# The mixing stage of a hybrid network written out tile by tile, with another order of steps on TensorE and VectorE

## What is computed

```
t = t + attn(ln(t))
t = t + ffn(ln(t))

def attn(inputs):                      # 8 heads of 16, 64 landmarks
    q, k, v = split(inputs @ Wqkv);  q = q * SCALE
    q_l, k_l = means of q, k over 16 tokens each
    attn1 = softmax(q @ k_l.T)         # 1024 x 64 per head
    attn2 = softmax(q_l @ k_l.T);  attn3 = softmax(q_l @ k.T)
    out = attn1 @ (pinv(attn2) @ (attn3 @ v)) + conv(v)
    return out @ Wout + bout

def ffn(x):                            # 2 shared experts, 8 routed, top 2
    probs = softmax(x @ gate_w.T + gate_b)
    top_v, top_i = top_k(probs, 2);  cw = top_v put at top_i, else 0
    routed = sum over e of cw[e] * (gelu(x @ rw1[e].T + rb1[e]) @ rw2[e].T + rb2[e])
    return shared(x) + sum(sb2) + routed
```

## Time and profile before

| | |
|---|---|
| three timed runs | 3307.7, 3250.42, 3266.44 us; median 3266.44 |
| profiled execution | 3237.99 us, of it the span of the profile 3235.9 us |
| mean granted clock of TensorE | 0.896 |
| PE busy | 2808.2 us (87%) |
| DVE busy | 2358.7 us (73%) |
| ACT busy | 1559.8 us (48%) |
| POOL busy | 1308.9 us (40%) |

### The profile page before, as it was taken

How to read it: one execution, slowest core, us unless ns; L and a number is a source line. 1 busy time by engine, 2 the same in 40 slices (tenths; PEclk the granted TensorE clock), 3 DMA queues, 4 the chain that set the end, 5 groups by cost and what they waited for, 6 DMA issues and landing times. The chain is left out here.

```text
span 3235.9 us, 96795 instructions
## 1 busy us (share of the span) xinstructions
PE 2808.2 (87%) x35815; PEld 2115.9 (65%) x35815; DVE 2358.7 (73%) x6126; ACT 1559.8 (48%) x3112; POOL 1308.9 (40%) x1616
## 2 busy tenths in 40 slices
PE   2999899997998899998888888887881999999998
PEld 1666666665776577777785666665661777767776
DVE  2687978885555688876776777677772877778888
ACT  1566756773443333331003333333330777778887
POOL 0476756774332111110001655555655000027776
PEclk6598969996999899998898987788885999999999
DMA  3011111110222000000000111111112444433333
GB/s 121 21 43 41 43 39 30 53 31 26 66 71 66 27 20 19 19 13 3 4 3 25 50 48 48 38 45 48 44 40 77 94 99 102 100 96 97 102 103 90
DMA packets 282520, 170.58 MB, mean 53 GB/s; under 512 B 94716, under 2 KB 269192, under 8 KB 281864
## 3 DMA queue, kind: packets, MB, share of 16 engines
q1 hardware_dynamic: 265736, 131.53, 14.9%
q0 software_dynamic: 16384, 33.59, 3.6%
HBM read 75.13 MB, written 71.30 MB: 45 GB/s over the span
## 5 line engine op out<-in xcount | busy, mean ns | idle before, releaser
L2303 DVE TENSOR_TENSOR e_glo<-e_g,e_ghi 128x512 f16<-128x512 f32 x540 | 374.8, 696 | 130.0 <-ACT e_ghi L2210 121.7
L2189 POOL DMA_INDIRECT e_got<-ys_dram,e_idx x256 | 254.9, 996 | 484.8 <-DMA ys_dram<-e_yo 401.2
L2205 ACT ACTIVATE e_g<-psum,b 128x512 f32<-128x512 f32 x540 | 371.1, 687 | 153.1 <-PE psum L2359 134.1
L2376 PE MATMUL psum<-w2hi,e_ghi 128*128 (+1 forms) x2160 | 389.8, 219 | 4.8 <-DVE e_glo L2303 4.7
L2378 PE MATMUL psum<-w2lo,e_ghi 128*128 (+1 forms) x2160 | 389.6, 219 | 0.0
L2380 PE MATMUL psum<-w2hi,e_glo 128*128 (+1 forms) x2160 | 389.6, 219 | 0.0
L1738 POOL DMA_INDIRECT xs_dram<-m_xt,m_idxl x256 | 264.3, 1032 | 110.9 <-issue 72.3
L2376 PEld LDWEIGHTS psum<-w2hi,e_ghi 128*128 128x128 f16 x2160 | 211.3, 98 | 73.2 <-DVE e_glo L2303 11.6
L2378 PEld LDWEIGHTS psum<-w2lo,e_ghi 128*128 128x128 f16 x2160 | 211.4, 98 | 60.9
L485 POOL TENSOR_TENSOR pT<-pT,rpbx 128x512 f32<-128x512 f32 x128 | 162.8, 1272 | 197.6 <-ACT pT L533 197.6
L2210 ACT ACTIVATE e_ghi<-psum,b 128x512 f16<-128x512 f32 x334 | 227.3, 680 | 0.0
(11 more groups left out here) (329 smaller groups left out, 7502.5 us busy)
## 6 DMA issues: line engine op xcount, KB each, us to landing
ys_dram<-e_yo SPq DMA_DIRECT2D x71, 256.0 KB
xT<-in_xT SPq DMA_DIRECT2D x16, 512.0 KB, 3.8
xw<-in_x SPq DMA_DIRECT2D x16, 512.0 KB, 5.1
f_xm<-x_dram SPq DMA_DIRECT2D x32, 256.0 KB, 2.9
mid_dram<-f_xm SPq DMA_DIRECT2D x32, 256.0 KB
l_t<-mid_dram SPq DMA_DIRECT2D x16, 512.0 KB
m_t<-mid_dram SPq DMA_DIRECT2D x16, 512.0 KB
res_dram<-m_rest SPq DMA_DIRECT2D x16, 512.0 KB
```

The lines of the kernel that those rows point to most:

```text
L2189: gp.indirect_dma_start(out=got[:, q % 2, k, t, :], out_offset=None, in_=ys, in_offset=bass.IndirectOffsetOnAxis(idx[:, q // 2, i:i + 1], 0))\
L2205: ac.activation(g32[:, c % 4, :], bank(c % 4), ACT.Gelu, bias=bias, scale=1.0 / WSCALE)\
L2303: ve.tensor_tensor(glo[:, c % 4, :], g32[:, c % 4, :], ghi[:, c % 4, :], ALU.subtract)\
L2376: pe.matmul(o, ghi[:, c % 4, g], w2hi[:, e, f, :], start=first and t == 0, stop=False, skip_group_check=True)
```

## The change

`phase_mix` is written anew. It still works tile by tile with a function `step(j)` on each engine, but the loop is gone: all 157 steps stand written out in each engine's program (`steps`). What is computed is the same.

On PE a step j now has the transposes of tile j, the scores of tile j+3 (before: j+2), the transpose of the normalised rows of tile j-2 (before: j-1), the sums of tile j-1 (before: j) and the output projection of tile j-3 (before: j-1). The exponentials have four buffers in place of two, their transposes one PSUM bank in place of two, and the projection has a bank of its own (5) in place of half of bank 0. The projection now takes the tokens from `lnT`, so that the copy `m_lt` is gone.

On DVE a step begins with the normalising of tile j-1, then the addition of tile j-4, the maximum of tile j+2, the statistics, the subtraction of tile j+2 and the statistics' mean (`bn_aggr`, before in a batch of eight per image).

ACT's step has the copy of the normalised rows of tile j-3, the copy of the exponentials' transposes of tile j and the exponential of tile j+1. ACT also takes over the normalisation of the tokens (from DVE, with scale and bias from two columns; DVE makes the bias, `m_nmr`), the keys of the heads (from DVE, eight instructions in place of one) and the copy of `zA` (from POOL), and it writes the 16-bit tokens to their place itself (before through `m_xh` and a copy by POOL).

The top 2 are now found by a maximum, a comparison with it and a choice of the first of equals, twice, in 12 operations on all eight tiles at once, in place of 16 comparisons of 8 x 8 and seven further operations. The experts' bias takes one transpose of all weights (66 columns with two of ones for the shared experts) and two products with a table `b2` of 66 x 1024, in place of eight transposes and eight products, so that POOL's addition of the shared bias is gone. POOL issues two scatters in each of eight steps (before 16 in six steps).

The diff, cut to the parts that move or change work:

```diff
-                lt = two("m_lt", [P, T])
...
-                e1 = sb("m_e1", [P, 2, AH, LM])
+                e1 = sb("m_e1", [P, 4, AH, LM])
...
+                        def step(j):
+                            q = j - 3
+                            if tile_at(q):
+                                met(ac, onT_ps, q)
+                                met(ac, w_ps, q - 2)
+                                ac.activation(onT[:, q % 2, :], bank(0)[:, 0:P], ACT.Copy)\
+                                    .then_inc(onT_ok.sem, 1)
+                            if tile_at(j):
+                                met(ac, eT_ps, j)
+                                met(ac, o_ps, j - 2)
+                                ac.activation(p1T[:, j % 2].rearrange("p a c -> p (a c)"), bank(4), ACT.Copy)\
+                                    .then_inc(eT_ok.sem, 1)
+                            q = j + 1
+                            if tile_at(q):
+                                met(ac, d_ok, q)
+                                ac.activation(e1[:, q % 4], e1[:, q % 4], ACT.Exp).then_inc(e_ok.sem, 1)
...
+                            b = image(j, 12)
+                            if b is not None:
+                                known(ac, nmr_ok, b)
+                                known(ac, xf_ps, b - 1, 2)
+                                known(ac, xtok_ok, b - 1)
+                                for t in range(NP):
+                                    ac.activation(xn[:, t, :], t2[b % 2][:, t, :], ACT.Identity, bias=nmr[:, t:t + 1],
+                                                  scale=rstd[:, t:t + 1]).then_inc(xn_ok.sem, 1)
...
+                                    ac.activation(xf[:, s], bank((1, 7)[u]), ACT.Copy)
+                                    ac.activation(x16[:, b, s], bank((1, 7)[u]), ACT.Copy).then_inc(hi_ok.sem, 1)
...
+                        def choose(b, k, p, n):
+
+
+                            best = wts[:, b, k * NP:k * NP + NP]
+                            ve.tensor_reduce(best, p[:], X, ALU.max).then_inc(gate.sem, 1)
+                            known(ve, gate, b, n + 1)
+                            ve.tensor_tensor(same[:], p[:], wide(best), ALU.is_equal).then_inc(gate.sem, 1)
+                            known(ve, gate, b, n + 2)
+                            ve.tensor_tensor(same[:], same[:], falling[:].unsqueeze(1).to_broadcast([P, NP, NE]), ALU.mult)\
...
+                            known(ve, gate, b, n + 3)
+                            ve.tensor_reduce(pick[:], same[:], X, ALU.max).then_inc(gate.sem, 1)
+                            known(ve, gate, b, n + 4)
+                            ve.tensor_tensor(sel[:, k], same[:], wide(pick[:]), ALU.is_equal).then_inc(gate.sem, 1)
...
-                            for t in range(NP):
-                                other = lg[:, t, :].unsqueeze(1).to_broadcast([P, NE, NE])
-                                own = lg[:, t, :].unsqueeze(2).to_broadcast([P, NE, NE])
-                                i1 = ve.tensor_tensor(eq[:, t], other, own, ALU.is_equal)
-                                i2 = ve.tensor_tensor(gt[:, t], other, own, ALU.is_gt)
...
-                            if j.real():
-                                normed(j)
-                            if j.t == 1 and w.real():
-                                positions(w)
-                            if (j - 1).real():
-                                add_out(j - 1)
...
-                            if j.t == 2 and y.real():
-                                known(ve, rstd_ok, y)
-                                known(ve, xtok_ok, y - NP)
-                                for t in range(NP):
-                                    ve.tensor_scalar(xn[:, t, :], t2[y.odd][:, t, :], mv[:, t, 0:1], rstd[:, t:t + 1],
-                                                     ALU.subtract, ALU.mult).then_inc(xn_ok.sem, 1)
...
+                            q = j - 1
+                            if tile_at(q):
+                                met(ve, o_ps, q)
+                                o = sums.rearrange("p (h d) -> p h d", h=AH)
+                                ve.reciprocal(r1[:, q % 2, :], o[:, :, AD]).then_inc(r_ok.sem, 1)
+                                met(ve, r_ok, q)
...
+                                ve.tensor_tensor(on[:, q % 2, :].rearrange("p (h d) -> p h d", h=AH), o[:, :, 0:AD],
+                                                 r1[:, q % 2, :].unsqueeze(2).to_broadcast([P, AH, AD]), ALU.mult)\
+                                    .then_inc(on_ok.sem, 1)
+                            q = j - 4
+                            if tile_at(q):
+                                met(ve, w_ps, q)
+                                known(ve, tb_ok, q // NP)
+                                known(ve, b_ok, q // NP - 2, 2)
+                                ve.tensor_tensor(t2[q // NP % 2][:, q % NP, :], bank(5)[:, 0:P],
+                                                 t_in[q // NP % 2][:, q % NP, :], ALU.add).then_inc(t2_ok.sem, 1)
+                            n = j + 2
+                            if tile_at(n):
+                                met(ve, s_ps, n)
+                                ve.tensor_reduce(m1[:, n % 2, :], scores_at(n), X, ALU.max).then_inc(mx_ok.sem, 1)
+                            if tile_at(q):
+                                met(ve, t2_ok, q)
...
+                            if tile_at(n):
+                                met(ve, mx_ok, n)
+                                met(ve, eT_ps, n - 4)
+                                ve.tensor_tensor(e1[:, n % 4], scores_at(n),
+                                                 m1[:, n % 2, :].unsqueeze(2).to_broadcast([P, AH, LM]), ALU.subtract)\
+                                    .then_inc(d_ok.sem, 1)
+                            if tile_at(q):
+                                met(ve, st_ok, q)
+                                ve.bn_aggr(mv[q // NP % 2][:, q % NP, :], st[:, q % NP, :]).then_inc(mv_ok.sem, 1)
...
+                            b = image(j, 12)
+                            if b is not None:
+                                known(ve, rstd_ok, b)
+                                ve.scalar_tensor_tensor(out=nmr[:], in0=mv[b % 2][:, :, 0], scalar=-1.0, in1=rstd[:], op0=ALU.mult,
+                                                        op1=ALU.mult).then_inc(nmr_ok.sem, 1)
...
+                        def weights_first(b):
+
+                            known(pe, gate, b, G)
+                            known(pe, qT_ok, b + 3, 2)
+                            pe.transpose(bank(1)[0:NP * NE + 2, 0:P], cwl[:], ident[:]).then_inc(cwT_ps.sem, 1)
...
+                            known(pe, cwT_ok, b)
+                            known(pe, qT_ok, b + 3, 2)
+                            known(pe, hi_ok, b, 2)
+                            for u in range(2):
+                                i = pe.matmul(bank((1, 7)[u]), cwT[:], b2[:, 512 * u:512 * u + 512], start=True, stop=True)
+                            i.then_inc(b_ps.sem, 1)
...
+                            q = j + 3
+                            if tile_at(q):
+                                b = q // NP
+                                known(pe, qT_ok, b, 2)
...
+                                met(pe, d_ok, q - 2)
+                                pe.matmul(bank(2 + q % 2), qT[b % 2][:, (q % NP) * P:(q % NP + 1) * P],
+                                          klm[b % 2][:].rearrange("p h l -> p (h l)"), start=True, stop=True).then_inc(s_ps.sem, 1)
...
+                            q = j - 2
+                            if tile_at(q):
+                                met(pe, on_ok, q)
+                                met(pe, onT_ok, q - 1)
+                                pe.transpose(bank(0)[:, 0:P], on[:, q % 2, :], ident[:]).then_inc(onT_ps.sem, 1)
...
                             q = j - 1
-                            if q.real():
-                                met(pe, on_ok, q)
-                                met(pe, t2_ok, q - 1)
-                                pe.transpose(bank(0)[:, 0:P], on[:, q.r, :], ident[:]).then_inc(onT_ps.sem, 1)
...
+                            if tile_at(q):
+                                met(pe, eT_ok, q)
+                                known(pe, zd_in, q // NP, 2)
...
-                            if q.real():
+                            q = j - 3
+                            if tile_at(q):
                                 met(pe, onT_ok, q)
-                                pe.matmul(bank(0)[:, C:2 * C], onT[:, q.r, :], wout[:], start=True, stop=False)
...
-                        tiles(pe, step)
+                                met(pe, t2_ok, q - 1)
+                                w = bank(5)[:, 0:P]
+                                pe.matmul(w, lnT[:, q // NP, (q % NP) * P:(q % NP + 1) * P], wvc[:], start=True, stop=False)
+                                pe.matmul(w, onT[:, q % 2, :], wout[:], start=False, stop=True).then_inc(w_ps.sem, 1)
```

(70 more changed lines are left out.)

561 lines of the change are left out of this document (214 added, 347 removed).

## The result

The changed kernel took 3383.85 us (median of 4 runs, 3354.2 to 3416.0); the kernel before, run beside it, 3258.43. The ratio is 1.040, with a 95% interval of 1.024 to 1.055: slower by 4%. The ratio is that of the faster executions of both kernels, so it is not quite that of the medians. The range held the time, but the time lies where the first rival was, not at the forecast of 3306, and the range reached that far only because this rival set its upper end.

What follows compares the result with a forecast made beforehand. PE was taken to run tiles without gaps, waiting at a few places per image. Images at 47.7 us, 1.8 more, gave +25; first two images +13, start +2, tail 0: +40 on 3266.4, so 3306 us; range 3235 to 3400.

Steps and rivals of the forecast that it cites:

- the first rival: Mixing stage: PE's clock falls to 0.71, an image takes 53.6 us, 3396 us in all; chance 0.28.
- The wait in every step: PE's projection of tile j-3 waits for DVE's addition of tile j-4, behind the sums just issued: 1.08 us per step.
- The plain step of 3.86 us: A tile's step on PE at full clock, without once-per-image work: 2.78 us before plus 1.08 us of wait.
- The normalisations on ACT: Eight token normalisations per image moved from DVE to ACT: 495 ns each, 3.1 us for eight with overlap.
- The stop of 3.4 us per image: PE waits for ACT's copy, which stands behind the eight token normalisations: 3.4 us per image, 1.7 at the lower bound.
- The clock: PE's mean granted clock in the mixing stage, taken as 0.87 against 0.84 before.
- The price of a hundredth: Each hundredth of PE's clock lost adds 0.37 us to an image of the mixing stage, 42.9 us at full clock.
- The argument against it: Against the lower clock: the first two images, with DVE idle 0.40 us behind the sums, ran at 0.97.
- the 20: Cost of the ends of the loop's four passes: some 20 us, 11.9 in stops and about as much by the clock.
- Start and tail: Stage start 2 us later by the head keys on ACT; tail after the last tile unchanged, within 4 us.
- DVE's room in its step: DVE needs 2.3 us of a 3.86 us step, leaving 1.5 us for gate work, which hangs over in four steps.
- The terms of 0.7 and 1.5 us: Per image: four PSUM copies ahead of ACT's copy, 0.7 us; DVE's gate work hanging over, 1.5 us, bounds 0 and 3.

Runs made afterwards that it cites:

- the run with all three edits: Changed kernel with DVE's addition and its maximum and subtraction ahead of the normalising, and ACT's normalisations behind the next copy and exponential: 3113.85 us, 0.962 against the kernel before.

## Why the prediction was right, and what in it was wrong

*The wait in every step: right.* It was priced at 1.08 us; the timeline shows 1.09, and 122 waits. The plain step of 3.86 us is 3.83 where the wait stands alone. A second wait was overlooked: normalising first also puts DVE's subtraction behind the sums, and so the scores of the next step. With both waits the step of the tile shown above took 4.33 us; without the second the stage was 34 us shorter, in one profile each.

*The normalisations on ACT: right in size.* The group of the changed kernel by line, as in the earlier trace rows:

```profile
L1762 ACT ACTIVATE m_xn<-m_t,m_nmr,m_rstd 128x128 f32<-128x128 f32 x128 | 50.9, 480 | 65.9 <-DVE m_nmr L1914 65.9
```

480 ns for 495, and 3.18 us for a row of eight for 3.1. The stop of 3.4 us per image is up to 3.8, and shorter where PE comes late at half clock; without it the stage is 47 us shorter. The Trainium skill's rule ("ScalarE: Activation LUTs", Rules for kernel authors) that adding and multiplying belong on VectorE agrees with the speeds here: 480 ns on ACT for 376 on DVE. But the loss came from the place and not from the engine, since the run with all three edits has the eight on ACT too, behind the next step's copy, and is the fastest.

*The clock: the step that failed.* The forecast took 0.87, because "the new gaps are short" and only the stop of 3.4 us would lower it. Measured were 0.73 in the images from the third on, and 0.78 in the first two, for which no loss was reckoned. With the 0.73 a sign of being wrong that the prediction had named, a clock under 0.78, came true. The price of a hundredth, 0.37 us, held: 42.9 + 27 x 0.37 = 52.9 us, and 53.1 were measured; the two neighbouring images above differ by 5.4 us for 15 hundredths, 0.36 each. So the miss is 14 hundredths, 5.2 us in each of 13.875 images, 72 us, and 14 in images 1 and 2 (85.9 for 72), against 5 and 6 us that the start and the tail came out shorter. The first rival, with 0.71, 53.6 us per image and 3396 us, is what happened; it had a chance of 0.28. The argument against it was the earlier trace rows: gaps of 0.40 us in the first images, at 0.97. Those gaps were no evidence, since they were DVE's idle time and not PE's.

*Why the clock fell: shown.* It is the gap, not the stop: filled with useless products it gives 0.94 with the stop in place, put into the old order it gives 0.75, and the stop taken away alone gives 0.77. The stop matters when the gap is gone (0.86 against 0.96). Why the clock stays low is argued and not shown: the projection's gap is 0.92 us at either clock, so PE at half clock is interrupted as often and as long, while with the addition first the scores' wait went from 1.15 to 0.24 us at half clock, and that stage had 0.87. The Trainium skill names a pattern of this kind ("TensorE: Matmul & The Clock Gate", A second HAM failure mode: psum-queue depth-cycling): short idle times between groups of products, often enough, make the clock swing between its levels. This case agrees, 0.69 and 0.84 in neighbouring images of the windows above. The sentence in Part 4 of that page of the Trainium skill, that transposes don't count as busy in the same way, was tested by no run; 0.96 was reached with four transposes in every tile.

*The other terms.* With the loop written out its stops are gone, 11.9 us of the 20; the rest of the 20 is not shown. Start and tail came out 2.9 and 6.4 us shorter, where +2 and 0 were written. DVE's room in its step was not the limit: DVE itself waited 406 us for PE's sums. The terms of 0.7 and 1.5 us were not measured by themselves. Two slips stand in the sums: the lower end of the range by its own terms is 3266 - 24 = 3242 and not 3235, and the stops were 3 us each (11.9 us in 4), not 4. Neither touches the forecast.

*Open.* Why the stop by ACT, with no gap, lowers the clock to 0.86, while it was 0.94 with the gap filled, was not settled: with the filling PE also had more to do in every step, and PE's idle time in the stage was nearly the same, 78 and 75 us. Whether the number of the gaps or the idle time in all decides was not separated either: PE was idle in the stage for 115 us before at 0.85, for 161 us in the changed kernel at 0.74, and for 112 us with the addition first at 0.87. Nor was the kernel before taken apart: its 0.85 holds with the loop written out (0.86).

## What to carry to other kernels

Before moving an operation to a later step, look at what stands ahead of it in the other engine's step: a wait is free only if the engine that ends it can start before the waiting engine has issued its last product. Here a wait in series with PE's own product cost more than its length: it was 0.92 us at either clock, and the clock of the stage fell with it. A wait for something that was started earlier shrank at half clock, from 1.15 to 0.24 us. When the time of a stage follows its clock, forecast the clock from the idle time of PE itself, and test the cause by filling the gap: if more work makes the stage faster, the gap is the cause.

## What was not expected of the hardware

A second, useless product of the scores in each tile, 243 more matrix instructions in the trace, made the stage 118 us faster, the clock going from 0.74 to 0.94. And one added wait per tile in the kernel before, 1.04 us in the mean (131.5 us in 126 waits), took its stage from 0.85 to 0.75 of full clock, although the stage's idle time grew by only 39 us. The prediction had taken gaps of this length for harmless to the clock.
